# Routed expert layer of a fused network on one core: early loads for its first half, four own PSUM banks, one product per bias group, and the next layer's first steps moved into it

## What is computed

```python
x = x + jnp.tanh(g_xattn[0]) * _L0_xattn_ref(_layernorm(x, axis=-1), ctx_768, ...)
x = x + jnp.tanh(g_ffn[0])   * _L0_ffn_ref(_layernorm(x, axis=-1), Wg, bg, W1, b1, W2, b2)
x = x + jnp.tanh(g_xattn[1]) * _L1_xattn_ref(_layernorm(x, axis=-1), ctx_768, ...)
```

## Time and profile before

| | |
|---|---|
| median of 3 runs | 1563.78 us (1562.2 to 1568.27) |
| profiled execution | 1562.19 us, its span 1560.5 us |
| mean granted TensorE clock | 0.934 of full speed |
| busy: PE, PEld, DVE, ACT, POOL | 87%, 67%, 70%, 59%, 44% |
| first attention | to 393 us |
| routed layer | 393 to 511 us |
| prologue of the second attention | 511 to 524 us |
| second attention, its 32 steps | 524 to about 770 us |

### The profile page before, as it was taken

One profiled execution on the slowest core, in us unless ns is written; L12 is line 12 of the kernel. 1 busy time (PEld: TensorE's weight loads), 2 busy tenths in 40 slices (PEclk: granted clock), 3 DMA queues, 4 the chain that ended last, 5 costly groups with the idle time before them and its releaser, 6 DMA issues.

```text
span 1560.5 us, 50076 instructions
## 1 busy us (share of the span) xinstructions
PE 1353.4 (87%) x17703; PEld 1043.6 (67%) x17735; DVE 1088.2 (70%) x4573; ACT 928.2 (59%) x2020; POOL 686.8 (44%) x1336
## 2 busy tenths in 40 slices
PE   6999999998466577788779699998999999999998
PEld 5888888886446344444466456666777777788886
DVE  6887878975113499999958734435889989866664
ACT  6566666655232567787513255554688888865553
POOL 3655555676430678676346311103434333334331
PEclk9999999999665789999989889997999999999999
DMA  7040000000452800000020100000000000000000
GB/s 175 3 119 0 0 0 3 6 15 16 134 155 69 189 15 21 0 0 0 2 66 0 35 1 0 0 0 1 3 3 0 0 2 3 3 9 7 7 15 21
DMA packets 66609, 42.77 MB, mean 27 GB/s; under 512 B 24589, under 2 KB 62954, under 8 KB 66346
## 3 DMA queue, kind: packets, MB, share of 16 engines
q1 hardware_dynamic: 64426, 36.78, 9.4%
q0 software_dynamic: 2048, 4.20, 0.9%
HBM read 28.38 MB, written 12.58 MB: 26 GB/s over the span
## 4 chain that ended last, share of the span: by engine, by line
PE 36%; DVE 17%; issue 7%; ACT 6%; POOL 3%; another core or an unknown queue 2%; DMA 2%; DVEq 1%; POOLq 0%; SPq 0%; ACTq 0%
DVE arena L1952 4%; PE ps L774 4%; PE ps L783 4%; DVE arena L1946 3%; PE ps L2672 3%; PE ps L2679 3%; PE ps L2753 2%; PE ps L2666 2%; PE ps L2722 2%; PE ps L2733 2%; PE ps L2741 2%; PE ps L2825 2%; DMA arena<-f_outs,arena 1%; PE ps L2794 1%
## 5 line engine op out<-in xcount | busy, mean ns | idle before, releaser
L3185 POOL TENSOR_TENSOR arena<-arena 128x512 f32<-128x512 f32 x64 | 67.8, 1059 | 112.8 <-DVE arena L3109 112.8
L1952 DVE MATCH_REPLACE8 arena<-arena 128x64 f32<-128x64 f32 x512 | 101.9, 211 | 0.1
L2431 DVE TENSOR_SCALAR_CACHE_REDUCE thr_hits<-thr_abs,thr_candidate 128x512 bf16<-128x512 f32 (+1 forms) x248 | 101.8, 479 | 0.0
L1946 DVE MAX8 arena<-arena 128x8 f32<-128x64 f32 x512 | 76.3, 212 | 8.8 <-POOL arena L1828 5.4
L2672 PE MATMUL ps<-arena,toeplitz 96*128 96x128 f32 x512 | 71.9, 284 | 9.7 <-ACT arena L2904 4.7
L667 POOL TENSOR_TENSOR ln_veps<-ln_mv,eps 128x4 f32<-128x4 f32 x32 | 9.1, 284 | 156.1 <-DVE ln_mv L661 156.1
L615 POOL TENSOR_TENSOR arena<-arena 128x1024 f32<-128x1024 f32 x32 | 61.4, 1918 | 34.2 <-DVE arena L556 34.2
L537 DVE TENSOR_REDUCE arena<-ps 128x16 f32<-128x1024 f32 x32 | 39.1, 1223 | 51.7 <-PE ps L356 51.6
L783 PEld LDWEIGHTS ps<-arena,toeplitz 128*128 128x128 f32 x512 | 63.5, 192 | 16.0 <-issue 13.4
L2672 PEld LDWEIGHTS ps<-arena,toeplitz 96*128 96x128 f32 x512 | 63.5, 195 | 15.4 <-ACT arena L2904 10.2
L385 PEld LDWEIGHTS ps<-arena 128*64 128x64 f32 x1024 | 60.3, 140 | 19.4 <-issue 11.1
(11 more groups left out here) (456 smaller groups left out, 4207.8 us busy)
## 6 DMA issues: line engine op xcount, KB each, us to landing
arena<-L_ffn_packed SPq DMA_DIRECT2D x48, 128.5 KB, 2.1
toeplitz<-ssm_toeplitz_scratch SPq DMA_DIRECT2D x2, 2048.0 KB, 18.1
f_rows<-arena SPq DMA_DIRECT2D x2, 1536.0 KB, 9.5
arena<-f_rows SPq DMA_DIRECT2D x12, 256.0 KB, 2.6
f_outs<-arena SPq DMA_DIRECT2D x12, 256.0 KB, 2.2
ssm_toeplitz_scratch<-ssm_padded_kernel SPq DMA_DIRECT2D x1, 2048.0 KB, 11.5
out<-x_res SPq DMA_DIRECT2D x8, 256.0 KB, 2.3
arena<-ctx SPq DMA_DIRECT2D x2, 768.0 KB, 5.8
```

The source lines that it names most:

```text
L1946: ins = V.max(m8[:, r, h, :], src[:, s, h, :])
L1952: ins = V.match_replace(W2[:, s, h, :], m8[:, r, h, :], src[:, s, h, :], TAKEN)
L2431: ins = V.tensor_scalar(self.hits[:, j, at:at + n], self.abs[:, at:at + n], self.cand[:, c:c + 1].bitcast(F32), 0.0, ALU.is_ge, ALU.add, a ...
L3185: G_.tensor_tensor(probs, probs, rc[:, s, :].unsqueeze(2).to_broadcast([P, heads, CTX]), ALU.mult).then_inc(s_prob.sem, 1)
```

## The change

- **Early loads.** Expert matrices of the first half's chunks 0, 1 and 2 are loaded during the first attention, as soon as the numbers are chosen and each place in memory is free (`queries_full`, `scores_full`); all expert numbers of the first half are read then. Rows 0 to 2, and chunk 3, follow when the scatters have landed; chunks 4 and 5 when the attention is done. The six chunks have six places.
- **Second half.** Its chunks lie in `k.toep` (four places for matrices, three for rows), free once the state-space kernel is summed; so `dve_sum` moves ahead of the biases, and `sp_matrices` waits for the last `outputs`. Chunk `c` waits as one for rows and matrices (`chunk_in`).
- **Stores** are issued by ACT, right behind `keep`, not by SP.
- **Banks.** Rows, hidden, outputs use one PSUM bank each (4, 5, 6), and the bias bank 7 (with 2, 4 and 5 where they are free); ACT does `gelu` before the next `lay`.
- **Order.** The router's last tiles (`pe_late`, `act_late`) stand behind the first chunk's `turn`; `pe_rank`, the weights and the biases stand between the chunks.
- **Biases.** The weights of a half are turned by one transpose, and a group is one product of 32 rows with a 32x512 block matrix `L0_ffn_b2_blocks` made on the host (256 KB to load, 4 KB before).
- **Next prologue.** `dve_prep` and the first two tiles' norm, turn, keys and query of the second attention stand inside the second half.
- **Gathers.** Six tiles (`AHEAD`) instead of 16 are gathered and added before the second attention; 26 come in 13 pairs inside it, and `late_tiles` has 16 steps written out instead of 12.

```diff
-    for t in range(12):
+    for t in range(16):
         step(t, t % 2)
-    with eng.Fori(6, 14) as it:
+    with eng.Fori(8, 14) as it:
...
+    AHEAD = 6
+    WEIGHT_RING, ROW_RING = 4, 3
...
     def sp(self, e):
+        N, C = range(GT), self.CHUNKS
+        e.wait_ge(self.chosen.sem, 1)
+        self.sp_expert(e, 0, 0, [self.sp_number(e, 0, 0, j) for j in N])
+        later = [[self.sp_number(e, 0, c, j) for j in N] for c in range(1, C)]
+        e.wait_ge(self.queries_full.sem, self.queries_full.end)
+        self.sp_expert(e, 0, 1, later[0])
+        e.wait_ge(self.scores_full.sem, self.scores_full.end)
+        self.sp_expert(e, 0, 2, later[1])
         e.wait_ge(self.scattered[0].sem, 16 * self.HALF)
+        for c in range(3):
+            self.sp_rows(e, 0, c)
+        self.sp_expert(e, 0, 3, later[2])
+        self.sp_rows(e, 0, 3)
         e.wait_ge(self.freed.sem, self.freed.end)
+        for c in range(4, C):
+            self.sp_expert(e, 0, c, later[c - 1])
             self.sp_rows(e, 0, c)
+
+        e.wait_ge(self.chosen.sem, 2)
+        e.wait_ge(self.k.ssm.summed.sem, 2)
+        self.sp_expert(e, 1, 0, [self.sp_number(e, 1, 0, j) for j in N])
+        e.wait_ge(self.scattered[1].sem, 16 * self.HALF)
+        self.sp_rows(e, 1, 0)
+        for c in range(1, C):
+            e.wait_ge(self.st_full.sem, C + c - self.ROW_RING + 1 if c >= self.ROW_RING else c + 1)
+            self.sp_rows(e, 1, c)
+            if c >= self.WEIGHT_RING:
+                e.wait_ge(self.o_full.sem, C + c - self.WEIGHT_RING + 1)
+            self.sp_expert(e, 1, c, [self.sp_number(e, 1, c, j) for j in N])
...
     def pe(self, e):
+        bias = lambda g: lambda e: self.pe_bias(e, g)
+        rank = lambda e: self.pe_rank(e, 1, self.k.ps[:, 1, 0:self.E * (self.HALF + 1)])
+        self.pe_chunks(e, 0, {0: [rank], 1: [lambda e: self.pe_weights(e, 0)], 2: [bias(0)], 3: [bias(1), lambda e: self.pe_weights(e, 1)], 4: [bias(2)], 5: [bias(3)]},
+                       lambda: self.pe_late(e))
+        self.prologue["pe"][0](e)
+        self.pe_chunks(e, 1, {3: [self.prologue["pe"][1]], 4: [self.prologue["pe"][2], bias(4)], 5: [bias(5)]})
+        bias(6)(e)
+        bias(7)(e)
+        self.prologue["pe"][3](e)
+        e.wait_ge(self.b_added.sem, GROUPS)
...
     def sp_matrices(self, e):
         e.wait_ge(self.summed.sem, 3)
+        e.wait_ge(self.toep_free.sem, self.toep_free.end)
```

More of the change, by code:

```diff
@@ L1371, in pe_chunks @@
         turn(0)
-        for c in range(self.CHUNKS):
+        if first:
+            first()
+        for c in range(C):
             hidden(c)
-            if c + 1 < self.CHUNKS:
+            if c + 1 < C:
                 turn(c + 1)
@@ L1405, in act_chunks, with pe_weights @@
-    def act_chunks(self, e, p):
-        S, ps = self.k.nc.scalar, self.k.ps
+            for step in after.get(c, ()):
+                step(e)
+        outputs(C - 1)
+    def pe_weights(self, e, p):
+        e.wait_ge(self.weighted.sem, p + 1)
+        e.wait_ge(self.l_laid.sem, TILES)
+        e.wait_ge(self.wt_laid.sem, p)
+        self.k.nc.tensor.transpose(self.k.ps[:, 3, 0:P], self.wgt[:, self.tiles(p), :].rearrange("p t e -> p (t e)"),
+                                   self.k.ident[:]).then_inc(self.wt_full.sem, 1)
@@ L1421, in act_chunks, with gelu @@
-        lay(0)
-        for c in range(self.CHUNKS):
-            n = p * self.CHUNKS + c
-            if c + 1 < self.CHUNKS:
-                lay(c + 1)
+            S.copy(self.rT[p][:, n % 2, :], ps[:, 4, :]).then_inc(self.sx_laid.sem, 1)
+        def gelu(c):
+            n = p * C + c
             e.wait_ge(self.h_full.sem, n + 1)
@@ L1428, in act_chunks, with keep @@
             for j in range(GT):
[L1429 to L1430 removed]
+                last = S.activation(self.hT[p][:, n % 2, j * P:(j + 1) * P], ps[:, 5, j * P:(j + 1) * P], ACT.Gelu,
+                                    bias=self.weights[n][:, j, 2 * D:2 * D + 1])
             last.then_inc(self.h_laid.sem, 1)
[L1432 to L1433 removed]
+        def keep(c):
+            n = p * C + c
+            e.wait_ge(self.o_full.sem, n + 1)
+            if c > 1:
+                e.wait_ge(self.stored[p][c % 2].sem, 16 * (c // 2))
+            S.copy(self.out[p][:, c % 2, :, :].rearrange("p j d -> p (j d)"), ps[:, 6, :]).then_inc(self.o_laid.sem, 1)
@@ L1434, in act_chunks, with store @@
+        def store(c):
+            e.wait_ge(self.o_laid.sem, p * C + c + 1)
+            e.dma_start(self.blocks(self.dst[p])[:, GT * c:GT * (c + 1), :], self.out[p][:, c % 2, :, :]).then_inc(self.stored[p][c % 2].sem, 16)
+        lay(0)
+        if first:
+            first()
+        for c in range(C):
+            gelu(c)
+            if c + 1 < C:
+                lay(c + 1)
             if c:
                 keep(c - 1)
-        keep(self.CHUNKS - 1)
-    def act_bias(self, e, g):
-        e.wait_ge(self.wt_full.sem, g + 1)
-        e.wait_ge(self.b_full.sem, g)
-        self.k.nc.scalar.copy(self.wT[0:self.E, :], self.k.ps[0:self.E, 6, :]).then_inc(self.wt_laid.sem, 1)
@@ new lines, in act_chunks, with act_weights, act_late @@
+            for step in after.get(c, ()):
+                step(e)
+        keep(C - 1)
+        store(C - 1)
+    def act_weights(self, e, p):
+        e.wait_ge(self.wt_full.sem, p + 1)
+        self.k.nc.scalar.copy(self.wT[:, p, :], self.k.ps[:, 3, 0:P]).then_inc(self.wt_laid.sem, 1)
+    def act_late(self, e):
+        k, ps, L = self.k, self.k.ps, self.LAST
+        for u in range(L + 1, TILES):
+            self.act_keep(e, u, u % 2)
+            self.act_turn(e, u, u % 2, ps[:, (u - L - 1) % 2, 0:P])
+        e.wait_ge(self.l_full.sem, TILES)
+        k.nc.scalar.copy(self.logit[:, L:TILES, :].rearrange("p t e -> p (t e)"), ps[:, 3, 0:4 * self.E]).then_inc(self.l_laid.sem, 4)
+        self.act_exp(e, 1)
@@ L1480, in dve @@
         self.dve_weigh(e, 1)
-        for g in range(GROUPS):
+        self.k.ssm.dve_sum(e)
+        for g in range(GROUPS // 2):
             self.dve_bias(e, g)
-        k.ssm.dve_sum(e)
-        e.wait_ge(self.gathered[0].sem, 16 * self.HALF)
-        for u in range(self.HALF):
+        self.prologue["dve"][0](e)
+        e.wait_ge(self.gathered[0].sem, 16 * self.AHEAD)
+        for u in range(self.AHEAD):
             self.dve_take(e, u)
+        self.prologue["dve"][1](e)
+        for g in range(GROUPS // 2, GROUPS):
+            self.dve_bias(e, g)
     def pool(self, e):
@@ L1976, in dve_step @@
         o = 1 - s
-        if isinstance(t, int) and 2 <= t < 10:
+        if isinstance(t, int) and 2 <= t < 2 + route.PAIRS:
             route.dve_pair(e, t - 2)
-        if isinstance(t, int) and t == 10:
-            e.wait_ge(before.sem, before.end)
         e.wait_ge(s_masked.sem, s_masked.at(t + 1))
@@ L1983, in dve_step @@
         topk_round(e, t, s, 0)
+        if isinstance(t, int) and 2 <= t < 16:
+            e.wait_ge(before.sem, min(route.AHEAD + 2 * t - 2, TILES))
+            e.nop(nofuse=True)
         if more(t, 4):
@@ L3285 @@
     arrays["L0_ffn_packed"] = np.ascontiguousarray(packed)
+    blocks = np.zeros((4, 4, 8, 4, D), np.float32)
+    for j in range(4):
+        blocks[:, j, :, j, :] = np.asarray(inputs["L0_ffn_b2"])
+    arrays["L0_ffn_b2_blocks"] = np.ascontiguousarray(blocks.reshape(P, 2, 2, D))
+    io["L0_ffn_b2_blocks"] = nc.dram_tensor("L0_ffn_b2_blocks", (P, 2, 2, D), F32, kind="ExternalInput").ap()
     io["L0_ffn_packed"] = nc.dram_tensor("L0_ffn_packed", packed.shape, F32, kind="ExternalInput").ap()
```

288 lines of the change are left out of this document (124 added, 164 removed).

## The result

| | before | changed |
|---|---|---|
| median of 4 runs | 1563.84 us (1562.2 to 1568.27) | 1523.43 us (1520.95 to 1527.12) |
| ratio | | 0.9753, interval 0.9724 to 0.9782 |
| span of the profiled execution | 1560.5 us | 1520.4 us |

What follows compares the result with a forecast made beforehand. PE was not the bound in the second half's first stretch: idle time beside indirect DMA trains, SP's list and the seam held it up. −40.6 (Toeplitz write) + 4.6 (pairs) = −36.0 us gave 1527 us; range 1511 to 1542.

Steps and rivals of the forecast that it cites:

- Seam: Routed layer to second attention: Toeplitz write goes out at 471.1 instead of 511.71, −40.6 us; what follows is counted from it.
- Last `outputs` at 471 (465 to 475): End of the routed layer's second half: chunk 5 complete at 458.5, then a tail of 12.5 us.
- rival 1: ACT idles through the scatter train as before; first half ends at 441, last `outputs` 474 to 484, total 1531 to 1540; chance 0.22.
- the tail: PE's work from chunk 5 complete to last `outputs`: 15.1 us at low clock, about 8.6 at high; taken as 12.5.
- The condition "costs nothing while the first half ends by 437": Second half, SP: chunk 0's `turn` must precede the rows of chunk 3; no delay claimed if the first half ends by 437.
- The blocks of 4.88 us throughout: Second half, SP: five blocks of rows, four readings and four matrices at 4.88 us each, 24.4 us, to 452.3.
- The six gathers, taken at 4.0: Second half: six gathers beside SP's last blocks cost it 4.0 us, scaled from 10.7 us for sixteen.
- Rival 5: Second attention, steps 10 to 14: each extra pair makes DVE wait 8.97 us, +45 instead of +4.6, +4 in all; chance 0.03.
- Prologue counted as nothing: Second attention's start: the shorter prologue, some 6 us, gains nothing because pair 0 stays behind the Toeplitz loads; bounds 0 and −6.
- rival 3: Second attention's start: gather pair 0 gets between the Toeplitz packets, gaining up to 6 us more, 1519 to 1524; chance 0.10.
- Thirteen pairs, +4.6: Second attention: five more steps with a pair, at POOL's 8.27 us instead of 7.35, cost +4.6 us, between 1.5 and 5.
- Stores: Routed layer: the stores' price is their place in SP's list, 2.2 to 2.5 us for each chunk, not just issuing.

Runs made afterwards that it cites:

- e4: Changed kernel with PE's mask transpose behind chunk 1 and SP reading expert numbers before waiting for the matrices' place: 1518.14 us, ratio 0.9723.
- e1: Changed kernel with the second half's 16 scatters in four groups, POOL waiting for each to land: 1521.97 us, ratio 0.9748.
- e2: Changed kernel with the second half's 16 indirect scatters replaced by plain writes, rows not sorted by expert: 1506.58 us, ratio 0.9654.
- e6: Changed kernel with all pieces of the next attention's prologue behind the last bias product on PE, ACT and DVE: 1521.15 us, ratio 0.9744.
- e5: Changed kernel with `AHEAD` 16 instead of 6, leaving 8 gather pairs instead of 13 for the second attention: 1523.36 us, ratio 0.9745.
- e11: Changed kernel with the second half's stores back in SP's list: 1524.94 us, ratio 0.9935 to a kernel before of 1535.4 us.
- e8: Changed kernel with scatters in two groups of eight, mask transpose behind chunk 1, expert numbers read earlier, Toeplitz loads late: 1506.23 us, ratio 0.963.

## Why the prediction was right, and where its steps failed

- **Seam.** That the Toeplitz write is the point to count from held: it carried 35.0 of the 40 us.
- **Last `outputs` at 471 (465 to 475): failed.** They ended at 476.65, inside rival 1. Of the 5.6 us that they came late, 4.4 came before chunk 5's `turn` (462.94 instead of 458.5) and 1.2 in the tail (13.7 instead of 12.5). The steps that failed are two. *The condition "costs nothing while the first half ends by 437"*: the half ended at 436.5, but the mask transpose waited 3.25 us more for DVE's preparation, so chunk 0's `turn` came at 439.86 and the rows of chunk 3 behind it. *The blocks of 4.88 us throughout*: the fourth took 7.6 us (446.67 to 454.24), because numbers are read behind the wait for a place (2.74 at PE), and the last 5.7; that was to be seen in the order of SP's list. The five blocks without the gathers' share took 30.0 us instead of 24.4. The six gathers, taken at 4.0, cost SP 1.1 (its matrices at 443.68 took 2.98 us instead of 1.88), which hid part of the miss. e4 took both waits away and moved the write to 469.5.
- **The idle time under the scatters.** 13.59 us, which I had left to a rival at 0.22 although all of the earlier trace rows spoke for it; e1 and e2 show that it was the unbroken scatters. It did not decide the total by itself: without it and with the scatters 6 us longer (e1) the last `outputs` end at 475.66.
- **Slips in my working.** Two thirds of the way from 8.6 to 15.1 is 12.9 and not 12.5. The ends of the loads (454.5 to 465) and of the tail (8.6 to 15.1) give 463 to 480 for the last `outputs`, wider than the 465 to 475 that I wrote, and 476.65 lies in it. Rival 5 with rival 1's last `outputs` at 474 to 484 gives +7 to +17, not +11 to +17.
- **Prologue counted as nothing: right on the total, wrong in the mechanism.** I priced the pieces inside the half at 2 us and said that pair 0 would come 35.6 us behind the write whatever happened. Measured: the pieces cost the half some 8 to 10 us (e6; the mask transpose's 3.25 is among them), and pair 0's first gather went out at 488.56, ahead of the loads at 489.17, so step 3 ended 5.6 us earlier than by the forecast. The two nearly cancel.
- **Pair 0 between the Toeplitz packets (rival 3).** The second gather of pair 0 was issued at 489.92 among the loads and had landed by 503.09, while they ran on to about 511: one gather in 13 us, the rate of the earlier trace rows (one in 12.7), not the 4.4 + 2 us of one large packet for each small one. So rival 3's mechanism came in part, by the first gather, which was issued ahead of the loads. The Trainium skill ("DMA: Bandwidth & Descriptors", section "Queues, rings and completion order") has a DMA engine go round-robin by packets; that a gather gets through at all agrees, its pace does not follow from it.
- **Thirteen pairs, +4.6: right.** 5.2 from step 3 to 14; POOL's pace 8.4 instead of 8.27; e5 gave it back (6.1).
- **Stores.** I read 2.2 to 2.5 us for each chunk from the earlier trace rows, in the list of the kernel before; in the changed list e11 shows some 12 us in the half. The wait ahead of a store in the list is the cost, as forecast. The Trainium skill ("DMA: Bandwidth & Descriptors", section "Issuing engines are not separate DMA queues") says that a second issuing engine saves sequencer time only; by that and the 0.43 us of an issue it would have been an estimated 0.4 each, and e11 does not agree.
- **Sizes.** -35.0 for -40.6, -5.6 for 0, +5.2 for +4.6, -4.4 behind step 31: that the sum of 36 came so close to the measured 40 is in part luck.

## What to carry to other kernels

An idle time that the profile can't explain is still a measurement: carry it into the sum as it stands, and let its disappearance be the rival. When a list is reordered, ask of every entry what it waits for and what stands behind that wait (readings of registers too), rather than giving blocks one pace. A bulk load whose reader comes 240 us later should not go out in front of small transfers that are due at once: one wait, 10 us.

## What the runs showed of the hardware

- **Long rows of indirect DMAs hold up other engines, on some chips.** On two chips ACT and PE stood idle, with inputs ready, from about the fifth of 16 DMAs issued 1.26 us apart until the last (PE busy 2.33 of 14 us), and SP took 9.87 us to issue four matrices. In groups of four they did not stand idle (11.64 of 14), with 16 plain writes in 8.6 us neither, and two groups of eight left 8.6 us. On a third chip the unbroken row cost nothing (e11: PE busy 14.00 of 14, four matrices issued in 1.89 us); the fourth has no trace of an unbroken row. The DMA engines were not full meanwhile (share 0.31). By what path it comes about, these runs do not show.
- **The kernel before has two times**: 1558.9 to 1567.3 us in 14 runs on the two chips of e1 to e8, and 1531.6 to 1540.9 in 29 runs on the other two. The traces place the difference: from the end of step 0 of the second attention to the end the kernel before took 1029.5 us on its chip, its version in fours 1029.1 and 1029.0 on the other two, and step 0 ended at 530.97 there, at 509.9 and 507.3 here. So all of it lies ahead of step 0, where the indirect DMAs of the routed layer are. The first attention was shorter too: its last add came at 386.91 in e11 and at 394.57 in the changed kernel, whose late steps with two scatters each took 11.9 to 12.4 us instead of 10.9 to 11.3. That the indirect DMAs make the whole difference is likely, but not shown, and as each chip ran at one time only, these runs do not part the chip from the time. A gain measured on one chip holds for that chip.
